# Cross-attention loop of a fused decoder layer: key and value units of two rounds issued in one block of the even round

## The chip, the cores and the metric

One NeuronCore of a Trainium2 chip runs the whole layer. The metric is the device time of one execution in microseconds (us); the kernel before was timed three times, and one further execution was profiled. The engines are named as the profile names them: PE (TensorE, with PEld for its weight loads), DVE (VectorE), ACT (ScalarE), POOL (GpSimd) and SP (SyncE, which here only issues transfers).

## What is computed

One pre-norm decoder layer on x (4 batches, 256 tokens, 128 channels): a local attention, a cross attention to a context of 512 tokens per batch, and two mixtures of 12 experts. The change lies in the cross attention, which per batch is, cut to what matters:

```python
lat = layer_norm(latents, ln_lat_g, ln_lat_b)
ctx = layer_norm(context, ln_ctx_g, ln_ctx_b)
q = (lat @ Wq).reshape(b, n, HEADS, DHEAD).transpose(0, 2, 1, 3)
k, v = jnp.split(ctx @ Wkv, 2, axis=-1)
k = apply_rope(k, cos, sin)
attn = jnp.einsum('bhnd,bhsd->bhns', q, k) * scale
attn = jax.nn.softmax(jnp.clip(attn, -11.0, 11.0), axis=-1)
out = jnp.einsum('bhns,bhsd->bhnd', attn, v) @ Wo + bo
```

There are 16 heads of 64 channels in each of 4 batches.

## The kernel before

The kernel writes one instruction stream per engine by hand, with semaphores between them. The cross attention is a loop of 32 rounds (`NPAIR`); a round is one pair of heads of one batch, and all five engines have their own copy of the loop. What the engines do in round r, in the order of their streams:

- **PE** (loop from L1311): the scores of the next pair, `scores(2r+2)` and `scores(2r+3)` (L1200, 16 matmul records each round); then the units: one value unit (`unit`, L1005 to L1007: 128 context tokens times 8 heads, for a round four later), one key unit (`key_products`, L1016 to L1018: all 512 tokens of the pair r+6), and in even rounds the queries of four heads (`queries`, L1134 to L1136); then the weighted values of this pair (`weigh_values`, L1219) and the sums of its weights (`sum_weights`, L1229). Units and queries use fp32r operands in three matmuls each (high and low parts), scores and values plain fp32.
- **ACT** (from L900): the exponentials of the next pair (`exponent`, L830, two of them), the copy of the value unit out of PSUM (`value_unit`, L739), in even rounds the copy of the queries (L821).
- **DVE** (from L1758): the division of the pair before (`divide`: reciprocal L1626, product L1630), the clips of the two exponentials (`clip`, L1619, in place), and the two reads of the key unit (`key_unit`: the sine part L1500, the cosine part L1505).
- **POOL** (from L611): two adds of the clipped weights (`weights_summed`, L573), one of the halves (`halves_summed`, L579), and the sum of the rotated key of pair r+4 (`key_sum`, L565), whose other half SP has swapped through SBUF by four transfers (`swap_halves`, L348).

What sets the order around the change are PSUM banks. Scores have banks 0 to 3, the outputs of pairs banks 4 and 7. **Bank 5** (`EXTRA_BANK`) takes the value units, and between them a turn of new latents or a projection of a finished batch (`extras`). **Bank 6** (`MISC_BANK`) takes the key units and the turned context of the next batch. `MISC` is the list of bank 6's users in order, and `misc_free(what)` makes PE wait until everything that stood in the bank before has been read:

```python
if MISC_NO[what]:
    pe.wait_ge(s["misc_read"], MISC_NO[what])
```

For a key unit the last read is DVE's cosine part L1505. In rounds 0, 6 and 14 the next batch's context is turned in bank 6 ahead of the key unit (`turn_context`, L979), read by ACT (`context_f`, L718, L724) and split by DVE (`context_lo`, L1491). In rounds 0 to 2, 9 to 11 and 14 to 16 DVE also normalizes the latents of the next batch in three parts (`latents`: statistics; L1445 and statistics; L1445), and POOL computes its square roots (L524, L525). Rounds 3, 12 and 17 end with the turn of these latents (L1112), rounds 11, 13, 19, 21, 27 and 29 with a projection (L1238) that DVE adds to x (`add_projected`, L1638). Rounds 22 on also carry the routing of the experts.

Of the kernel before, what the change touches and what calls it, by code (L numbers as in the profile page):

```python
# [7 lines left out]
P = 128  # L8
# [15 lines left out]
def decoder_layer(nc, x, ctx_in, pos, a_wq, a_wk, a_wv, a_wpost, a_wrel, a_pds,  # L24
# [77 lines left out]
    with ExitStack() as ctx:  # L102
# [115 lines left out]
        e_sb = sb("e_sb", [P, ERING, 2, KH, S], F32, second)  # L218
        v_sb.append(sb("v_sb1", [P, KC, HG, DX], F32, second))
        e_part = sb("e_part", [P, 2, 2, 2, S], F32, second)  # L220
# [68 lines left out]
        for r in range(NPAIR):  # L289
            if r + V_LEAD < NG * KC:  # L290
                ROUND_VALUES[r] = len(UNIT)
                UNIT.append(("v", r + V_LEAD))
# [10 lines left out]
        CONTEXT_ROUND = {0: 1, PPB - 2: 2, 2 * PPB - 2: 3}  # L303
# [17 lines left out]
        EXTRA_NO = {what: n for n, what in enumerate(EXTRA)}  # L321

# [189 lines left out]
        def _(pool):  # L512
# [137 lines left out]
        def _(act):  # L650
# [64 lines left out]
            def context_f(b):  # L715
                if b >= 1:
                    act.wait_ge(s["ctx_lo_done"], b)
                act.activation(ctx_f[:, :], bank(7 if b == 0 else MISC_BANK), ACT.Identity, scale=affine[:, 2:3], bias=affine[:, 3:4])\  # L718
                   .then_inc(s["misc_read" if b else "ctx_f_done"], 1)
                if b:  # L720
# [161 lines left out]
            outputs_turned(5)  # L882

# [16 lines left out]
            for r in range(NPAIR):  # L900
# [3 lines left out]
                if r in CONTEXT_ROUND:  # L904
                    misc_wait(("context", CONTEXT_ROUND[r]))
                    context_f(CONTEXT_ROUND[r])
                if r in ROUND_VALUES:
                    value_unit(ROUND_VALUES[r])
                if r % 2 == 0 and r // 2 + 1 < NQ:
                    queries_out(r // 2 + 1)  # L910
                if r in CONTEXT_NORM:
# [41 lines left out]
        def _(pe):  # L953
# [296 lines left out]
            local_project(2)  # L1250
            local_project(3)
# [46 lines left out]
            def route_1(i):  # L1298
                if i in ROUTE.values():
                    pe.wait_ge(s["v_done"], min(i // 2 + V_LEAD, NG * KC - 1) + 1)  # L1300
# [10 lines left out]
            for r in range(NPAIR):  # L1311
# [7 lines left out]
                if r in CONTEXT_ROUND:  # L1319
                    misc_free(("context", CONTEXT_ROUND[r]))  # L1320
                    turn_context(CONTEXT_ROUND[r], MISC_BANK, "misc_ps")
                if r in ROUND_VALUES:
                    route_read(2 * r - 2)
                    if extras.get(r - 1) in EXTRA_NO:
                        pe.wait_ge(s["extra_read"], EXTRA_NO[extras[r - 1]] + 1)
                    unit(ROUND_VALUES[r])
                if r + K_LEAD < NPAIR:
                    misc_free(("keys", r + K_LEAD))
                    key_products(r + K_LEAD, bank(MISC_BANK)).then_inc(s["misc_ps"], 1)
                if r % 2 == 0 and r // 2 + 1 < NQ:  # L1330
                    queries(r // 2 + 1)
                weigh_values(2 * r)
# [4 lines left out]
                if r in extras:  # L1337
                    what = extras[r]
                    if what in EXTRA_NO:
                        pe.wait_ge(s["v_done"], r + V_LEAD + 1)  # L1340
# [86 lines left out]
        def _(dve):  # L1427
# [313 lines left out]
            local_residual(3)  # L1741

# [7 lines left out]
            for r in range(NPAIR):  # L1750
                if r:
                    divide(r - 1)
                if r == NORM_ROUND:
# [11 lines left out]
                if r in CONTEXT_ROUND:  # L1765
                    context_lo(CONTEXT_ROUND[r])
# [4 lines left out]
                if r in extras:  # L1771
                    if extras[r][0] == "latents":
                        latents_lo(extras[r][1])
                    else:
                        add_projected(extras[r])
# [86 lines left out]
```

## Time and profile before

| | us |
|---|---|
| median of 3 runs (lowest to highest) | 430.64 (429.86 to 430.83) |
| the profiled execution, its own time | 430.4 |
| its span, first to last instruction | 428.5 |
| the loop: first scores of round 0 to the last values of round 31 | 61.50 to about 276.7 |
| busy in the span: PE, DVE, POOL, ACT | 402.4, 332.6, 260.0, 177.8 |

The granted TensorE clock is 1.00, the full 2.4 GHz, in every stretch. In a timeline row the first number is the start in us from the span's start, the second the duration, and a bracket at the end gives the idle time before the instruction with what ended it; rows of one kind that follow each other are merged, so "x2 1.92" is two instructions in 1.92 us. A matmul's duration contains its drain; the pace is read from start to start.

### The profile page before, as it was taken

How to read it: one execution, taken by the hardware profiler on the slowest of the kernel's cores; microseconds unless marked ns; L12 is line 12 of the kernel's file. 1: busy time of each engine (PE TensorE's matmuls, PEld its weight loads, DVE VectorE, ACT ScalarE, POOL GpSimd, SP SyncE). 2: the span in 40 equal slices, each digit the busy share in tenths (PEclk: the TensorE clock that was granted, in tenths of full speed). 3: DMA queues.
4: the chain of work that ended last, by engine and by line, in shares of the span. 5: the costliest groups of instructions: out<-in, count | busy, mean ns of one | idle time of the engine just before them, and what ended most of it. 6: DMA issues, size and time to landing. Idle time of an engine off the chain costs nothing.

```text
span 428.5 us, 8269 instructions
## 1 busy us (share of the span) xinstructions
PE 402.4 (94%) x3040; PEld 294.8 (69%) x3040; DVE 332.6 (78%) x655; ACT 177.8 (41%) x282; POOL 260.0 (61%) x225
## 2 busy tenths in 40 slices
PE   3988798989999999989999998999999999999996
PEld 2666675656677776757676675687767888888885
DVE  8888768998999978997788997886778861755544
ACT  6867354454464335443355435335257533000000
POOL 6823539999798988998979777767434850000000
PEclk9999999999999999999999999999999999999999
DMA  7696432131211111111201161547337730000000
GB/s 179 160 214 102 79 81 54 45 83 47 51 26 49 27 49 33 41 46 34 50 24 41 36 115 40 154 70 155 61 95 164 152 61 2 6 7 14 6 6 14
DMA packets 84746, 28.63 MB, mean 67 GB/s; under 512 B 71957, under 2 KB 79050, under 8 KB 84706
## 3 DMA queue, kind: packets, MB, share of 16 engines
q1 hardware_dynamic: 81748, 26.80, 28.3%
q10 hardware_dynamic: 2958, 1.30, 1.3%
q8 instruction: 25, 0.41, 0.4%
q14 instruction: 15, 0.12, 0.1%
HBM read 17.67 MB, written 2.02 MB: 46 GB/s over the span
## 4 chain that ended last, share of the span: by engine, by line
PE 66%; DVE 16%; SPq 7%; issue 4%; ACT 2%; DMA 2%; POOL 2%; DVEq 0%; ACTq 0%; POOLq 0%
PE psum L1219 10%; PE psum L1200 9%; PE psum L1402 5%; PE psum L1403 5%; PE psum L1401 5%; SPq L415 5%; PE psum L1362 4%; PE psum L1364 4%; PE psum L1363 4%; DVE rden L1626 4%; PE psum L1238 3%; PE psum L1229 3%; DVE e_sb L1619 2%; PE psum L1005 2%; PE psum L972 1%
## 5 line engine op out<-in xcount | busy, mean ns | idle before, releaser
L573 POOL TENSOR_TENSOR e_part<-e_sb 128x512 f32<-128x512 f32 x64 | 90.6, 1434 | 20.4 <-DVE e_sb L1619 20.4
L830 ACT ACTIVATE e_sb<-psum 128x1024 f32<-128x1024 f32 x64 | 62.2, 1022 | 85.0 <-PE psum L1200 82.9
L1200 PE MATMUL psum<-q_t,kT 64*128 64x256 f32 x512 | 64.2, 389 | 0.0
L1219 PE MATMUL psum<-e_sb,v_sb 128*64 128x256 f32 x512 | 63.8, 386 | 0.0
L1626 DVE RECIPROCAL rden<-psum 128x256 f32<-128x256 f32 x32 | 55.9, 1748 | 9.6 <-PE psum L1229 9.4
L1826 DVE SCALAR_TENSOR_TENSOR x_sb<-psum,dw,x_sb 128x128 f32<-128x128 f32 x96 | 33.7, 351 | 38.1 <-PE psum L1403 35.5
L1619 DVE TENSOR_SCALAR e_sb<-e_sb 128x1024 f32<-128x1024 f32 x64 | 58.6, 948 | 2.8 <-ACT e_sb L830 2.6
L1200 PEld LDWEIGHTS psum<-q_t,kT 64*128 64x128 f32 x512 | 46.7, 186 | 13.9 <-issue 8.4
L1219 PEld LDWEIGHTS psum<-e_sb,v_sb 128*64 128x64 f32 x512 | 33.7, 136 | 22.3 <-issue 6.3
L565 POOL TENSOR_TENSOR kT<-kT,raw 128x512 f32<-128x512 f32 x32 | 44.1, 1377 | 8.1 <-DMA raw<-rope_b 8.1
L602 POOL TENSOR_TENSOR xeT_lo<-xeT,xeT_hi 128x512 fp32r<-128x512 f32 x24 | 31.4, 1309 | 28.4 <-ACT xeT_hi L844 28.3
L579 POOL TENSOR_TENSOR e_part<-e_part 128x512 f32<-128x512 f32 x32 | 41.8, 1306 | 2.5
L1362 PE MATMUL psum<-xeT_hi,w1T_hi 128*128 128x512 f32 x96 | 38.9, 405 | 0.8 <-ACT h_f L946 0.5
L1402 PE MATMUL psum<-w2T_lo,h_hi 128*128 128x512 f32 x96 | 38.0, 396 | 0.0
L1403 PE MATMUL psum<-w2T_hi,h_lo 128*128 128x512 f32 x96 | 37.8, 394 | 0.0
L1364 PE MATMUL psum<-xeT_hi,w1T_lo 128*128 128x512 f32 x96 | 37.5, 391 | 0.0
L1363 PE MATMUL psum<-xeT_lo,w1T_hi 128*128 128x512 f32 x96 | 37.5, 390 | 0.0
L1401 PE MATMUL psum<-w2T_hi,h_hi 128*128 128x512 f32 x96 | 37.3, 389 | 0.0
L844 ACT ACTIVATE xeT_hi<-xeT 128x512 fp32r<-128x512 f32 x24 | 15.2, 632 | 29.4 <-DVE xeT L1669 21.3
L1362 PEld LDWEIGHTS psum<-xeT_hi,w1T_hi 128*128 128x128 f32 x96 | 18.0, 188 | 7.0 <-issue 2.6
L1500 DVE TENSOR_TENSOR rope_b<-psum,sinT 128x512 f32<-128x512 f32 x30 | 20.4, 679 | 2.1 <-PE psum L1018 2.1
L1505 DVE TENSOR_TENSOR kT<-psum,cosT 128x512 f32<-128x512 f32 x32 | 21.6, 676 | 0.0
(202 smaller groups left out, 729.9 us busy)
## 6 DMA issues: line engine op xcount, KB each, us to landing
raw<-rope_b SPq DMA_DIRECT2D x116, 64.0 KB, 2.0
w_raw<-in_L_ffn_W_dram SPq DMA_DIRECT2D x96, 64.0 KB, 2.3
gates<-gate_dram SPq DMA_DIRECT2D x6, 768.0 KB, 4.4
ctx_sb<-in_ctx_dram SPq DMA_DIRECT2D x4, 256.0 KB, 6.1
vbd<-v_dram SPq DMA_DIRECT2D x16, 52.6 KB
v_dram<-v_tok SPq DMA_DIRECT2D x4, 136.0 KB
raw<-in_L_xattn_Wkv_dram SPq DMA_DIRECT2D x2, 256.0 KB, 5.7
kT<-in_L_xattn_Wkv_dram SPq DMA_DIRECT2D x2, 256.0 KB, 4.7
```

Of the source, the lines that this page charges most:

```text
L573: pool.tensor_tensor(e_part[:, p % 2, half, :, :], e_sb[:, i % ERING, :, 0, :], e_sb[:, i % ERING, :, 1, :], ALU.add)\
L830: act.activation(e_sb[:, i % ERING, :, :, :].rearrange("p a k t -> p (a k t)"), psum[:, a:a + 2, :].rearrange("p a b -> p (a b)"), ACT.Exp ...
L1200: mm = pe.matmul(psum[:, 2 * (i % 2) + a, t * S:(t + 1) * S], key_slot(p)[rows, kt * P:(kt + 1) * P], q_t[rows, j % 2, p % 2, :], start=Tr ...
L1219: mm = pe.matmul(psum[DX * a:DX * a + DX, pv_bank(p), 0:S], v_sb[g % 2][:, kt, 2 * pp + a, :], e_sb[:, i % ERING, a, t, :], start=(kt == 0 ...
L1362: pe.matmul(bank(c), w1T_hi[:, e, c, :], hi, start=(e == 0), stop=False)
L1363: pe.matmul(bank(c), w1T_hi[:, e, c, :], lo, start=False, stop=False)
L1364: mm = pe.matmul(bank(c), w1T_lo[:, e, c, :], hi, start=False, stop=(e == NE - 1))
L1401: pe.matmul(o, hi, w_hi, start=(c == 0), stop=False)
L1402: pe.matmul(o, hi, w_lo, start=False, stop=False)
L1403: mm = pe.matmul(o, lo, w_hi, start=False, stop=(c == HC - 1))
L1619: dve.tensor_scalar(e, e, E_LO, E_HI, ALU.max, ALU.min).then_inc(s["clip_done"], 1)
L1626: dve.reciprocal(rden[:, p % 2, :], psum[:, pv_bank(p), S:2 * S]).then_inc(s["rden_done"], 1)
```

## The change

- Key and value units of rounds r and r+1 (r even) stand in round r. PE's even round becomes scores, value unit, key unit, queries, second value unit, second key unit, weighted values, sums. Its odd round has scores, weighted values and sums only.
- ACT copies the second value unit behind the queries of the even round; DVE does the reads of both key units one after the other behind the clips of the even round.
- Context 1 is turned ahead of the loop, in bank 6, behind `local_project(2)`. Contexts 2 and 3 are still turned in rounds 6 and 14, but behind the second key unit and in bank 5; DVE's `context_lo` for them stands in the round after.
- DVE adds a projection, or splits the latents' low part, behind the division of the round after, not ahead of it (save the last ones).
- Ahead of the loop, POOL's first sums of weights stand between the key sums, and no longer wait for all of x; for that two tiles (`e_part`, `v_sb1`) change places in memory.

```diff
-        for r in range(NPAIR):
-            if r + V_LEAD < NG * KC:
-                ROUND_VALUES[r] = len(UNIT)
-                UNIT.append(("v", r + V_LEAD))
+        for r in range(0, NPAIR - V_LEAD, 2):
+            ROUND_VALUES[r] = len(UNIT)
+            UNIT.extend([("v", r + V_LEAD), ("v", r + V_LEAD + 1)])
...
-        CONTEXT_ROUND = {0: 1, PPB - 2: 2, 2 * PPB - 2: 3}
+        CONTEXT_ROUND = {PPB - 2: 2, 2 * PPB - 2: 3}
...
-        MISC, EXTRA = [("queries", 0)], []
+        MISC, EXTRA = [("queries", 0), ("context", 1)], []
         for r in range(NPAIR):
             if r in CONTEXT_ROUND:
-                MISC.append(("context", CONTEXT_ROUND[r]))
-            if r + K_LEAD < NPAIR:
-                MISC.append(("keys", r + K_LEAD))
+                EXTRA.append(("context", CONTEXT_ROUND[r]))
+            if r % 2 == 0 and r + K_LEAD < NPAIR:
+                MISC.extend([("keys", r + K_LEAD), ("keys", r + K_LEAD + 1)])
...
-            for p in range(4):
-                key_sum(p)
-            pool.wait_ge(s["x1_done"], NT)
+            pool.wait_ge(s["lat_in_done"], TPB)
+            key_sum(0)
+            key_sum(1)
             weights_summed(0)
+            key_sum(2)
             weights_summed(1)
             halves_summed(0)
+            key_sum(3)
...
             local_project(2)
+            turn_context(1, MISC_BANK, "misc_ps")
             local_project(3)
...
-                if r in CONTEXT_ROUND:
-                    misc_free(("context", CONTEXT_ROUND[r]))
-                    turn_context(CONTEXT_ROUND[r], MISC_BANK, "misc_ps")
                 if r in ROUND_VALUES:
...
                     unit(ROUND_VALUES[r])
-                if r + K_LEAD < NPAIR:
+                if r % 2 == 0 and r + K_LEAD < NPAIR:
                     misc_free(("keys", r + K_LEAD))
                     key_products(r + K_LEAD, bank(MISC_BANK)).then_inc(s["misc_ps"], 1)
                 if r % 2 == 0 and r // 2 + 1 < NQ:
                     queries(r // 2 + 1)
+                if r in ROUND_VALUES:
+                    unit(ROUND_VALUES[r] + 1)
+                if r % 2 == 0 and r + K_LEAD < NPAIR:
+                    misc_free(("keys", r + K_LEAD + 1))
+                    key_products(r + K_LEAD + 1, bank(MISC_BANK)).then_inc(s["misc_ps"], 1)
+                if r in CONTEXT_ROUND:
+                    pe.wait_ge(s["v_done"], values_by(r))
+                    turn_context(CONTEXT_ROUND[r], EXTRA_BANK, "extra_ps")
...
                 if r:
                     divide(r - 1)
+                if extras.get(r - 1, "none")[0] == "project" and r - 1 < NPAIR - 3:
+                    add_projected(extras[r - 1])
...
-                if r + K_LEAD < NPAIR:
+                if r % 2 == 0 and r + K_LEAD < NPAIR:
                     key_unit(r + K_LEAD, MISC_BANK)
+                    key_unit(r + K_LEAD + 1, MISC_BANK)
```

How the instructions stand on PE from the units of an even round on, before (round 4 and the units of round 5; the lines are those of the kernel before):

```order
L1016 MATMUL psum<-ctx_hi,wkv_hi 128x512 [waits ctx_lo_done,misc_read]
...
L1136 MATMUL psum<-lat_hi,wq_lo 128x256
L1219 MATMUL psum<-e_sb,v_sb 64x256 [waits ox_done,v_done,clip_done]
...
L1200 MATMUL psum<-q_t,kT 128x256 x3
L1005 MATMUL psum<-wkv_hi,ctx_hi 128x512 [waits ctx_lo_done,v_done]
L1006 MATMUL psum<-wkv_lo,ctx_hi 128x512
L1007 MATMUL psum<-wkv_hi,ctx_lo 128x512
L1016 MATMUL psum<-ctx_hi,wkv_hi 128x512 [waits ctx_lo_done,misc_read]
L1017 MATMUL psum<-ctx_lo,wkv_hi 128x512
L1018 MATMUL psum<-ctx_hi,wkv_lo 128x512
```

and in the changed kernel (round 4 and the start of round 5; L1021 to L1023 are the value unit, L1032 to L1034 the key unit, L1150 to L1152 the queries, L1235 the weighted values):

```order
L1032 MATMUL psum<-ctx_hi,wkv_hi 128x512 [waits ctx_lo_done,misc_read]
...
L1152 MATMUL psum<-lat_hi,wq_lo 128x256
L1021 MATMUL psum<-wkv_hi,ctx_hi 128x512 [waits ctx_lo_done,v_done]
L1022 MATMUL psum<-wkv_lo,ctx_hi 128x512
L1023 MATMUL psum<-wkv_hi,ctx_lo 128x512
L1032 MATMUL psum<-ctx_hi,wkv_hi 128x512 [waits ctx_lo_done,misc_read]
L1033 MATMUL psum<-ctx_lo,wkv_hi 128x512
L1034 MATMUL psum<-ctx_hi,wkv_lo 128x512
L1235 MATMUL psum<-e_sb,v_sb 64x256 [waits ox_done,v_done,clip_done]
```

The second value and key unit moved up from the odd round, behind the queries; the second key unit waits on the same `misc_read` that DVE raises after the first.

On DVE, rounds 10 and 11 before (a round's rows are from its reciprocal to the next one):

```order
L1626 RECIPROCAL rden<-psum 128x256 [waits ox_done,den_ps]
L1630 TENSOR_TENSOR o_t<-psum,rden 128x256 [waits rden_done]
...
L1619 TENSOR_SCALAR e_sb<-e_sb 128x1024 [waits exp_done] x2
L1500 TENSOR_TENSOR rope_b<-psum,sinT 128x512 [waits keys_done,misc_ps]
L1505 TENSOR_TENSOR kT<-psum,cosT 128x512 [waits score_ps]
L1638 TENSOR_TENSOR x_sb<-psum,x_sb 128x128 [waits extra_ps]
L1626 RECIPROCAL rden<-psum 128x256 [waits ox_done,den_ps]
```

and in the changed kernel from the clips of round 10 on (L1644 is the clip, L1525 and L1530 the reads of a key unit, L1651 and L1655 the division, L1663 the added projection):

```order
L1644 TENSOR_SCALAR e_sb<-e_sb 128x1024 [waits exp_done] x2
L1525 TENSOR_TENSOR rope_b<-psum,sinT 128x512 [waits keys_done,misc_ps]
L1530 TENSOR_TENSOR kT<-psum,cosT 128x512 [waits score_ps]
L1525 TENSOR_TENSOR rope_b<-psum,sinT 128x512 [waits keys_done,misc_ps]
L1530 TENSOR_TENSOR kT<-psum,cosT 128x512 [waits score_ps]
...
L1651 RECIPROCAL rden<-psum 128x256 [waits ox_done,den_ps]
L1655 TENSOR_TENSOR o_t<-psum,rden 128x256 [waits rden_done]
L1663 TENSOR_TENSOR x_sb<-psum,x_sb 128x128 [waits extra_ps]
L1644 TENSOR_SCALAR e_sb<-e_sb 128x1024 [waits exp_done] x2
```

Both key units are read behind the clips of the even round, and the projection is added behind the division.

## Rows read from the trace of the kernel before

**Rows 1.** Rounds 6 to 17: PE, PEld, DVE, ACT, POOL busy, granted clock, DMA.

```profile
103.90:185.20 81.30, 80.19 (x586) 56.16 (x584) 74.98 (x101) 37.87 (x52) 72.14 (x56) 1.00 0.15 38
```

**Rows 2.** Timeline of PE, round 5 and the units of round 6.

```profile
98.08 2.00 PE L1200 MATMUL psum<-q_t,kT 64*128 64x256 f32 x16
100.01 0.50 PE L1005 MATMUL psum<-wkv_hi,ctx_hi 128*128 128x512 f32 x1
100.35 0.40 PE L1006 MATMUL psum<-wkv_lo,ctx_hi 128*128 128x512 f32 x1
100.58 0.39 PE L1007 MATMUL psum<-wkv_hi,ctx_lo 128*128 128x512 f32 x1
...
101.59 1.95 PE L1219 MATMUL psum<-e_sb,v_sb 128*64 128x256 f32 x16
103.90 2.00 PE L1200 MATMUL psum<-q_t,kT 64*128 64x256 f32 x16
...
107.75 0.51 PE L1016 MATMUL psum<-ctx_hi,wkv_hi 128*128 128x512 f32 x1 [0.56 <-ACT ctx_f L718]
...
108.56 0.28 PE L1134 MATMUL psum<-lat_hi,wq_hi 128*128 128x256 f32 x1
...
109.35 1.95 PE L1219 MATMUL psum<-e_sb,v_sb 128*64 128x256 f32 x16
```

**Rows 3.** Who PE waited for, 61.5 to 274.7 us: us in total, times, longest.

```profile
PE psum L1134 <- DVE o_t L1630: 4.8, 5, 1.5
PE psum L1016 <- ACT ctx_f L718: 1.7, 3, 0.6
PE psum L1229 <- POOL e_part L579: 1.0, 1, 1.0
```

**Rows 4.** Timeline of PE and ACT: score starts of rounds 19, 20, 25; exponentials of 19.

```profile
193.13 2.00 PE L1200 MATMUL psum<-q_t,kT 64*128 64x256 f32 x16
...
200.96 2.00 PE L1200 MATMUL psum<-q_t,kT 64*128 64x256 f32 x16
...
236.19 2.00 PE L1200 MATMUL psum<-q_t,kT 64*128 64x256 f32 x16
...
194.31 1.94 ACT L830 ACTIVATE e_sb<-psum 128x1024 f32<-128x1024 f32 x2 [2.78 <-PE psum L1200]
```

**Rows 5.** Timeline of DVE, rounds 19, 20 and 25.

```profile
195.38 1.92 DVE L1619 TENSOR_SCALAR e_sb<-e_sb 128x1024 f32<-128x1024 f32 x2
...
197.83 0.67 DVE L1505 TENSOR_TENSOR kT<-psum,cosT 128x512 f32<-128x512 f32 x1
...
205.32 0.68 DVE L1505 TENSOR_TENSOR kT<-psum,cosT 128x512 f32<-128x512 f32 x1
...
239.35 1.69 DVE L1619 TENSOR_SCALAR e_sb<-e_sb 128x1024 f32<-128x1024 f32 x1 [0.22 <-ACT e_sb L830]
...
241.56 0.67 DVE L1505 TENSOR_TENSOR kT<-psum,cosT 128x512 f32<-128x512 f32 x1
```

**Rows 6.** Timeline of POOL and DVE around round 17's clips (182.30), one instruction a row.

```profile
181.51 1.29 POOL L579 TENSOR_TENSOR e_part<-e_part 128x512 f32<-128x512 f32 x1
182.30 1.05 DVE L1619 TENSOR_SCALAR e_sb<-e_sb 128x1024 f32<-128x1024 f32 x1
182.76 1.72 POOL L565 TENSOR_TENSOR kT<-kT,raw 128x512 f32<-128x512 f32 x1
...
183.27 1.76 DVE L1619 TENSOR_SCALAR e_sb<-e_sb 128x1024 f32<-128x1024 f32 x1
```

**Rows 7.** POOL's adds, 95 to 240 us: shortest, median, longest in ns.

```profile
L573 POOL TENSOR_TENSOR e_part<-e_sb x43: 1257/1277/1797, 95.6 to 239.2; 128x512 f32<-128x512 f32 x43
```

**Rows 8.** Timeline of DVE, parts of the latents' normalization, and round 0's clips.

```profile
132.10 2.30 DVE L1445 TENSOR_SCALAR xn<-x_sb,mv,rstd 128x128 f32<-128x128 f32 x2
...
175.19 1.57 DVE L1445 TENSOR_SCALAR xn<-xn,mv,rstd 128x128 f32<-128x128 f32 x2
...
63.73 3.19 DVE L1619 TENSOR_SCALAR e_sb<-e_sb 128x1024 f32<-128x1024 f32 x2 [0.31 <-ACT e_sb L830]
```

More of the change, by code:

```diff
@@ L218, in decoder_layer @@
         e_sb = sb("e_sb", [P, ERING, 2, KH, S], F32, second)
+        e_part = sb("e_part", [P, 2, 2, 2, S], F32, second)
         v_sb.append(sb("v_sb1", [P, KC, HG, DX], F32, second))
-        e_part = sb("e_part", [P, 2, 2, 2, S], F32, second)
         rden = sb("rden", [P, 2, S], F32, second)
@@ L288, in decoder_layer, with values_by @@
         ROUND_VALUES = {}
-        for r in range(NPAIR):
-            if r + V_LEAD < NG * KC:
-                ROUND_VALUES[r] = len(UNIT)
-                UNIT.append(("v", r + V_LEAD))
+        for r in range(0, NPAIR - V_LEAD, 2):
+            ROUND_VALUES[r] = len(UNIT)
+            UNIT.extend([("v", r + V_LEAD), ("v", r + V_LEAD + 1)])
+        def values_by(r):
+            return min(r - r % 2 + V_LEAD + 2, NG * KC)
         UNIT_BANK += [5] * (len(UNIT) - len(UNIT_BANK))
@@ L321, in decoder_layer, with extra_before @@
         EXTRA_NO = {what: n for n, what in enumerate(EXTRA)}
+        def extra_before(r):
+            at = [EXTRA_NO[what] for q in range(r) for what in (("context", CONTEXT_ROUND.get(q)), extras.get(q)) if what in EXTRA_NO]
+            return max(at, default=-1) + 1
         def key_slot(p):
@@ L717, in context_f @@
                     act.wait_ge(s["ctx_lo_done"], b)
-                act.activation(ctx_f[:, :], bank(7 if b == 0 else MISC_BANK), ACT.Identity, scale=affine[:, 2:3], bias=affine[:, 3:4])\
-                   .then_inc(s["misc_read" if b else "ctx_f_done"], 1)
-                if b:
+                act.activation(ctx_f[:, :], bank((7, MISC_BANK, EXTRA_BANK, EXTRA_BANK)[b]), ACT.Identity, scale=affine[:, 2:3], bias=affine[:, 3:4])\
+                   .then_inc(s[("ctx_f_done", "misc_read", "extra_read", "extra_read")[b]], 1)
+                if b >= 2:
+                    act.wait_ge(s["extra_read"], EXTRA_NO["context", b] + 1)
+                elif b:
                     act.wait_ge(s["misc_read"], MISC_NO["context", b] + 1)
@@ L882, in _ @@
             outputs_turned(5)
+            misc_wait(("context", 1))
+            context_f(1)
             def context_normalize(b):
@@ L903, in _ @@
                     exponent(2 * r + 3)
-                if r in CONTEXT_ROUND:
-                    misc_wait(("context", CONTEXT_ROUND[r]))
-                    context_f(CONTEXT_ROUND[r])
                 if r in ROUND_VALUES:
@@ L910, in _ @@
                     queries_out(r // 2 + 1)
+                if r in ROUND_VALUES:
+                    value_unit(ROUND_VALUES[r] + 1)
+                if r in CONTEXT_ROUND:
+                    act.wait_ge(s["extra_ps"], EXTRA_NO["context", CONTEXT_ROUND[r]] + 1)
+                    context_f(CONTEXT_ROUND[r])
                 if r in CONTEXT_NORM:
@@ L1299, in route_1 @@
                 if i in ROUTE.values():
-                    pe.wait_ge(s["v_done"], min(i // 2 + V_LEAD, NG * KC - 1) + 1)
+                    pe.wait_ge(s["v_done"], values_by(i // 2))
                 if i == ROUTE["weights"]:
@@ L1339, in _ @@
                     if what in EXTRA_NO:
-                        pe.wait_ge(s["v_done"], r + V_LEAD + 1)
+                        pe.wait_ge(s["v_done"], values_by(r))
+                        if EXTRA_NO[what]:
+                            pe.wait_ge(s["extra_read"], EXTRA_NO[what])
                     else:
@@ L1741, in _ @@
             local_residual(3)
+            context_lo(1)
             beside = {6: (output_bias, 0), NPAIR - 6: (output_bias, 1)}
@@ L1760, in _ @@
                     clip(2 * r + 3)
-                if r + K_LEAD < NPAIR:
+                if r % 2 == 0 and r + K_LEAD < NPAIR:
                     key_unit(r + K_LEAD, MISC_BANK)
+                    key_unit(r + K_LEAD + 1, MISC_BANK)
                 if r == NORM_ROUND:
                     final_norm(0, 1)
-                if r in CONTEXT_ROUND:
-                    context_lo(CONTEXT_ROUND[r])
+                if r - 1 in CONTEXT_ROUND:
+                    context_lo(CONTEXT_ROUND[r - 1])
                 if r in beside:
@@ L1770, in _ @@
                 route_1(2 * r)
[L1771 to L1775, printed above, removed]
+                if extras.get(r - 1, "none")[0] == "latents":
+                    latents_lo(extras[r - 1][1])
+                if r in extras and r >= NPAIR - 3:
+                    add_projected(extras[r])
                 route_1(2 * r + 1)
```

8 lines of the change are left out of this document (5 added, 3 removed).

## The prediction

> **What bounds the kernel now.** I read the busy time by stretch first. In rounds 6 to 17 PE is busy 80.2 of 81.3 us, DVE 75.0 and POOL 72.1, the clock at its full 2.4 GHz [rows 1]. So the loop is PE's, with two engines close behind. PE's timeline then gives the cost of a round. Scores take 1.93 us (98.08 to 100.01), the units of an odd round 1.58 (to 101.59), weighted values and sums 2.31 (to 103.90) [rows 2]. Inside the units a matmul of 512 columns follows the one before by 0.23 (100.35 to 100.58), so a unit is 0.70; the queries are 0.70 too (108.56 to 109.35 is 0.79, with the way out below). Six matmuls would be 1.40, so going from fp32 into fp32r and back costs 0.18 per round, 0.11 of it on the way in (100.01 to 100.35 against 0.23) [rows 2]. Last, the list of waits: in the loop PE waits for the division 4.8 us in five places, for a turned context 1.7 in three, once 1.0 for the first sums [rows 3]. After a wait the first unit takes 0.81 and not 0.70 (107.75 to 108.56) [rows 2], so I add 0.1 to each.
>
> **What is taken away.**
> - *Blocks.* Rounds 1, 3, ... 27, fourteen of them, lose their way in and out: 14 x 0.18 = 2.5.
> - *Contexts.* The three waits go, since context 1 is turned in a gap ahead of the loop and the others behind the units: 1.7 + 0.3 = 2.0. The transposes themselves stay.
> - *Division first.* The queries of an even round wait for the division of the pair before. DVE's odd round is now shorter by one key unit, and an added projection no longer stands ahead of the division: 4.8 + 0.5 = 5.3, if all five waits go.
> - *First sums.* POOL does them between the key sums: 1.0.
>
> Together 10.8. POOL's, ACT's and SP's work is the same; the swaps of a key are issued a round earlier or later, with four rounds until POOL needs it, and cost nothing. The exchanged tiles cost nothing.
>
> **What is added.** PE's second key unit writes bank 6, and `misc_free` holds it until DVE has finished the cosine part of the first. Before, that read had a whole round; now it has what stands between the two key units on PE, queries and a value unit, 1.40 us. Behind the waiting unit on PE stand this pair's weighted values and sums and the next scores; behind those wait DVE's next division and ACT's next exponentials. So every us of this wait is a us of the loop, in the 13 rounds 0, 2, ... 24.
>
> Without a wait the second key unit would start 1.93 + 0.11 + 4 x 0.70 = 4.84 us after the round's scores. When is DVE done? In its order stand division, two clips, two reads. In round 19, where DVE had been idle, the clips start 2.25 after the scores (195.38 against 193.13), the exponentials 1.18 after (194.31), and the cosine part ends at 198.50, 5.37 after [rows 4, 5]. Round 20 is the shortest with 5.04 (200.96 to 206.00), round 25 the longest with 6.04 (236.19 to 242.23) [rows 4, 5]. All are later than 4.84. With 0.06 for the signal and 0.1 for the restart the wait costs at least 5.04 + 0.06 - 4.84 + 0.1 = **0.36** and by these rows at most 1.36.
>
> I expect more, because clips and POOL's adds exclude each other. A clip alone takes 0.60; in round 17 the first was issued at 182.30, ran only when POOL's add ended at 182.80, and the second stood from 183.27 to 185.03, until POOL's next add had ended at 184.48 [rows 6]. That add took 1.72 where 1.28 is the median of POOL's adds [rows 6, 7]. They take turns. In round 25 the second clip came 0.22 after the first and waited for an add too: 1.69 [rows 5].
>
> Now the cycle. In the odd round POOL has long been idle, so its four adds start behind the first clip, at 2.25 + 0.65 = 2.9 after the scores; with 0.6 for the second clip and 4 x 1.25 they end at 8.5. The odd round lasts only 1.93 + 2.31 = 4.24 on PE, so POOL adds until 4.3 us into the even round, across both clips. That is round 17's pattern: 2.73 for the pair of clips (182.30 to 185.03). Issued at 2.25 they end at 4.98, the two reads take 1.28 and end at 6.26, and the wait costs 6.26 + 0.06 - 4.84 + 0.1 = 1.6; a second clip of the odd round that runs late as in round 25 pushes the division by up to 0.45, which makes 2.0. I take the middle.
> - Rounds 4, 6, 8, 18, 24, behind a short odd round: 5 x 1.8 = 9.0.
> - Rounds 12, 14, 20, 22, behind an odd round with a projection (2 us longer, in which POOL catches up and only one add is in the way, as in round 25): 6.04 gives 1.36, so 4 x 1.4 = 5.6.
> - Rounds 2, 10, 16, where a part of the latents' normalization (1.6 to 2.3, with its statistics up to 3.0 [rows 8]) stands ahead of the clips on DVE; some 0.9 of it falls into time that DVE would wait for the second exponential: 3 x 3.0 = 9.0.
> - Round 0: clips of 3.2 us among POOL's key sums, 63.73 to 66.92, now behind the context's low part [rows 8]; with the reads 68.2, 6.7 after the scores at 61.5, with that part about 7.3: 2.5.
>
> Sum 26.1.
>
> The Trainium skill says in SBUF — State Buffer, section SBUF: two separate sides, that VectorE and GpSimd share one pair of ports under an exclusive lock, so that the one that comes second waits for the other's whole instruction. The rows of round 17 agree, 1.05 and 1.76 us against 0.60. By the rule, with every clip behind a full add, the five plain rounds would cost 2.0 and the sum would be 1.0 higher.
>
> **Sum.** 430.4 + 26.1 - 10.8 = 445.7 against the profiled execution; the median of the runs lies 0.2 above it, so **445.9**. Break-even is a mean wait of 10.8 / 13 = 0.83 us. Ends: with 0.36 in all 13 rounds 430.6 - 10.8 + 4.7 = 424.5; with 2.1, 1.9, 3.5 and 3.0 in the four groups (31.6) and one division wait left in round 2 (0.8), 452.2.
>
> **Rivals.**
> - *The cover nearly holds* (faster). The mechanism is the same place, `misc_free` ahead of the second key unit, with DVE at its earliest: POOL's adds fall between the clips, and the cosine part ends about 5.0 after the scores as in round 20. Then the wait is 0.36 and the time 424 to 429. It decides below 0.83. For it: DVE has 1.3 us more to itself in odd rounds. Against: three of three rounds read have 5.04 or more with POOL less late than it will be.
> - *The wait is that of the rows of before.* POOL's lag does not carry over, and the mean of 5.04, 5.37 and 6.04, 5.48, holds: 0.8 in nine rounds, 2.0 in the three with normalization, 2.5 in round 0, 15.7 in all: 435.5. This is no change or a little slower, around 430 to 438.
> - *The clock falls.* The Trainium skill says in TensorE: Matmul & The Clock Gate, The HAM clock gate, that an array left idle long enough runs at half speed until it has been busy again. As a mechanism here: the longest waits, about 3 us in rounds 2, 10 and 16, would be followed by the rest of their round (0.70 + 2.31) at 1.2 GHz, 3 us more each, and so 455. The rows show 1.00 with waits of up to 1.5 [rows 1, 3]; longer ones inside the loop no row here shows.
>
> That the change does not do what it says can be left out: the streams show the second units in the even round.
>
> **How the numbers follow.** Forecast 0.58 (438 to 452); the rows' own wait 0.24 (430 to 438); the cover nearly holds 0.13; the clock 0.05. The range 429 to 452 leaves out most of the third, the clock and the edges, about 0.2. A measurement of this kernel tells about 0.2% (0.9 us) from no change: faster 0.14, same 0.05, slower 0.81.
>
> **What would show it.** In the changed profile PE's list of waits should have the second key unit waiting for DVE's cosine part, some 13 times and about 25 us, as its largest entry, no wait for a turned context, and little for the division. In the timeline an even round should last 9.5 to 10 us and an odd one 4.2, and the clips of even rounds should stand behind POOL's adds. I am wrong if that wait is under 0.8 a round, if PE's odd rounds wait for something, or if the clock is under 1.00.

## The result, and the profile after

The changed kernel takes **454.42 us** (median of 4 runs, 452.91 to 456.61) against 430.74 of the kernel before (429.86 to 433.42): ratio 1.0543, 95% interval 1.0479 to 1.0606. Forecast were 445.9 and at most 452. The profiled execution took 456.61, its span is 454.7.

Two lines of the page after, busy time and the granted clock in 40 slices:

```profile
PE 411.7 (91%) x3040; PEld 298.0 (66%) x3040; DVE 334.5 (74%) x655; ACT 179.8 (40%) x282; POOL 256.9 (56%) x225
...
PEclk9999998899898899989999999999999999999999
```

PE is busy 9.3 us longer (402.4 before) with the same number of matmuls, DVE and ACT about 2 us longer, POOL 3 us less; the 8s are slices in which the clock fell. Who PE waited for, in the whole execution (us in total, times, longest):

```profile
PE psum L1032 <- DVE kT L1530: 22.5, 12, 4.2
...
PE psum L1150 <- DVE o_t L1655: 2.2, 2, 1.7
```

Against [rows 3]: the turned context and the first sums are gone, of the 4.8 us for the division 2.2 are left (rounds 26 and 28), and the key unit has come in as the largest entry: 21.9 us in ten rounds of the loop, the other two waits stand ahead of it. In rounds 14, 20 and 22 the second key unit is 0.27 us late, which the list does not count. One even round, PE's timeline from the second value unit of round 8 to the end of round 9 (start, duration):

```profile
131.41 0.40 PE L1021 MATMUL psum<-wkv_hi,ctx_hi 128*128 128x512 f32 x1
...
134.34 0.50 PE L1032 MATMUL psum<-ctx_hi,wkv_hi 128*128 128x512 f32 x1 [2.08 <-DVE kT L1530]
...
135.25 3.43 PE L1235 MATMUL psum<-e_sb,v_sb 128*64 128x256 f32 x16
...
139.24 2.00 PE L1216 MATMUL psum<-q_t,kT 64*128 64x256 f32 x16
141.17 1.95 PE L1235 MATMUL psum<-e_sb,v_sb 128*64 128x256 f32 x16
```

Two losses follow each other: 2.08 us of waiting, and then weighted values that take 3.43 us where they take 1.95 in round 9. Why the cosine part was late, DVE and POOL in round 8:

```profile
130.38 2.70 DVE L1644 TENSOR_SCALAR e_sb<-e_sb 128x1024 f32<-128x1024 f32 x2
133.01 0.68 DVE L1525 TENSOR_TENSOR rope_b<-psum,sinT 128x512 f32<-128x512 f32 x1
133.61 0.68 DVE L1530 TENSOR_TENSOR kT<-psum,cosT 128x512 f32<-128x512 f32 x1
...
129.55 1.29 POOL L587 TENSOR_TENSOR e_part<-e_part 128x512 f32<-128x512 f32 x1
130.80 1.73 POOL L573 TENSOR_TENSOR kT<-kT,raw 128x512 f32<-128x512 f32 x1
```

The two clips take 2.70 us among POOL's adds, as in [rows 6], and the reads stand behind them. Granted clock of whole rounds (length; PE, PEld, DVE, ACT, POOL busy; clock; share and GB/s of the DMA), rounds 4, 8 and 9, and 10, and last a stretch inside the weighted values of round 8:

```profile
96.88:106.55 9.67, 8.21 (x56) 5.62 (x55) 8.09 (x10) 4.61 (x7) 9.21 (x7) 1.00 0.12 29
...
127.14:139.24 12.10, 10.03 (x56) 6.27 (x55) 8.40 (x10) 5.16 (x9) 10.10 (x8) 0.86 0.09 22
139.24:143.48 4.24, 4.24 (x39) 2.81 (x37) 4.01 (x8) 1.94 (x2) 1.13 (x1) 1.00 0.26 66
143.48:156.62 13.14, 9.85 (x57) 6.37 (x55) 9.32 (x14) 3.62 (x5) 12.36 (x11) 0.87 0.08 20
...
136.00:138.00 2.00, 2.00 (x12) 1.09 (x10) 0.64 (x2) 0.00 (x0) 2.00 (x2) 0.50 0.01 1
```

Rounds 0, 2, 6, 8, 10 and 16 read 0.86 to 0.88, all others 1.00. The 0.50 is 1.2 GHz. From the second key unit to the next scores five of the six need 4.80 to 4.90 us, where rounds 4, 18 and 20 with 1.00 need 3.20 to 3.22; round 6, which also turns a context, needs 5.28 where round 14 needs 3.64: **1.65 us each, 9.9 in all.** Ahead of the second key unit each of the six had waited 1.84 to 4.16 us; round 4 waited 1.46 and kept its clock. The Trainium skill (TensorE: Matmul & The Clock Gate, The HAM clock gate) has it that an array left idle runs at half rate until it has been busy again; the 0.50 above agrees, and 16 matmuls in 3.43 for 1.95 us are near that.

**Where the time went**, from round 0's scores to round 30's (208.83 us before, 234.66 after): the second key unit starts 24.6 us later than it could (4.84 after the round's scores), summed over 13 rounds; 1.3 for the restarts; 9.9 for the clock; less 2.5 for the blocks. That leaves 7.5 for everything else taken away: 234.66 - 208.83 = 25.9 + 9.9 - 2.5 - 7.5. The 2.5 is the forecast's own figure and the 7.5 a remainder. Compared pair by pair of rounds, with the late start, the restart and the slow stretch taken off, the blocks give 0.20 in each of 14 pairs (2.8), the three contexts 2.2 and 0.4 more because the transposes of context 1 left the loop, the first sums 1.3, the division 3.3: together 10.0. A wait costs more than the list shows: round 4 of the kernel before lasts 8.17 us and round 8, which has none, 6.54, for a listed wait of 1.40.

### The profile page after: what moved, and what is told of

The parts are those of the page before. It is cut to its first block, busy times and chain, and to the rows that moved or that the text cites. A ratio compares the mean times of both kernels' runs of the same rounds, so it can differ in the third digit from the quotient of the medians.

```text
span 454.7 us, 8275 instructions
## 1 busy us (share of the span) xinstructions
PE 411.7 (91%) x3040; PEld 298.0 (66%) x3040; DVE 334.5 (74%) x655; ACT 179.8 (40%) x282; POOL 256.9 (56%) x225
## 4 chain that ended last, share of the span: by engine, by line
PE 58%; DVE 26%; issue 7%; ACT 4%; DMA 2%; ACTq 1%; POOL 1%; DVEq 0%; POOLq 0%
PE psum L1235 11%; PE psum L1216 6%; DVE e_sb L1644 6%; DVE rden L1651 5%; PE psum L1427 5%; PE psum L1428 5%; PE psum L1426 5%; PE psum L1387 4%; PE psum L1388 4%; PE psum L1389 4%; PE psum L1254 3%; PE psum L1245 2%; DVE xn L1470 2%; DVE rope_b L1525 2%; DVE kT L1530 2%
## 5 line engine op out<-in xcount | busy, mean ns | idle before, releaser
L581 POOL TENSOR_TENSOR e_part<-e_sb 128x512 f32<-128x512 f32 x64 | 87.6, 1381 | 46.0 <-DVE e_sb L1644 45.4
L1651 DVE RECIPROCAL rden<-psum 128x256 f32<-128x256 f32 x32 | 56.1, 1752 | 23.8 <-PE psum L1245 23.7
L1235 PE MATMUL psum<-e_sb,v_sb 128*64 128x256 f32 x512 | 71.9, 424 | 0.0
L1644 DVE TENSOR_SCALAR e_sb<-e_sb 128x1024 f32<-128x1024 f32 x64 | 65.3, 1043 | 7.0 <-ACT e_sb L842 6.9
L1235 PEld LDWEIGHTS psum<-e_sb,v_sb 128*64 128x64 f32 x512 | 37.1, 150 | 29.1 <-issue 17.2
L1032 PE MATMUL psum<-ctx_hi,wkv_hi 128*128 128x512 f32 x32 | 14.6, 457 | 23.0 <-DVE kT L1530 22.5
L1525 DVE TENSOR_TENSOR rope_b<-psum,sinT 128x512 f32<-128x512 f32 x30 | 20.6, 685 | 15.8 <-PE psum L1034 15.8
L1032 PEld LDWEIGHTS psum<-ctx_hi,wkv_hi 128*128 128x128 f32 x32 | 6.0, 187 | 30.4 <-DVE kT L1530 29.2
```

The source lines that it names most:

```text
L581: pool.tensor_tensor(e_part[:, p % 2, half, :, :], e_sb[:, i % ERING, :, 0, :], e_sb[:, i % ERING, :, 1, :], ALU.add)\
L1235: mm = pe.matmul(psum[DX * a:DX * a + DX, pv_bank(p), 0:S], v_sb[g % 2][:, kt, 2 * pp + a, :], e_sb[:, i % ERING, a, t, :], start=(kt == 0 ...
L1644: dve.tensor_scalar(e, e, E_LO, E_HI, ALU.max, ALU.min).then_inc(s["clip_done"], 1)
L1651: dve.reciprocal(rden[:, p % 2, :], psum[:, pv_bank(p), S:2 * S]).then_inc(s["rden_done"], 1)
```

## The experiments

The front part of the kernel, ahead of the loop, differs by up to 2.5 us between the profiled executions (the loop began at 59.89 to 62.44), and the number of rounds in which the clock fell does too (the same kernel, e3 below: span 428.0 us at a mean clock of 1.000, 434.0 at 0.984). So mechanisms are compared by the stretch from round 0 to 30 of the profiled executions, and kernels by their medians. The ratios of e1 to e11 are to executions of the kernel before made beside them, with medians of 431.1 to 431.4 and mean clocks of 0.991 to 0.999; 430.74 and 208.83 are of the executions of the result.

| kernel | median us | ratio to before (95%) | rounds 0 to 30 | mean clock |
|---|---|---|---|---|
| before | 430.74 | | 208.83 | 1.000 |
| as changed | 454.42 | 1.0543 (1.0479 to 1.0606) | 234.66 | 0.977 |
| e1 keys apart | 429.20 | 0.9951 (0.9930 to 0.9971) | 206.91 | 1.000 |
| e2 before, merged | 453.53 | 1.0562 (1.0487 to 1.0638) | 229.74 | 0.985 |
| e3 read first | 432.94 | 1.0047 (1.0010 to 1.0084) | 213.48 | 0.984 |
| e4 filled | 447.43 | 1.0381 (1.0335 to 1.0426) | 224.86 | 0.998 |
| e6 parts behind | 429.44 | 0.9967 (0.9945 to 0.9989) | 207.32 | 0.996 |
| e7 short adds | 430.50 | 0.9975 (0.9944 to 1.0006) | 206.91 | 1.000 |
| e8 key inside | 428.04 | 0.9928 (0.9908 to 0.9949) | 206.76 | 0.999 |
| e9 parts odd | 427.31 | 0.9909 (0.9878 to 0.9941) | 206.04 | 0.999 |
| e10 odd, last | 426.54 | 0.9895 (0.9857 to 0.9933) | 204.03 | 0.999 |
| e11 apart, odd, last | 429.58 | 0.9969 (0.9944 to 0.9995) | 208.04 | 0.998 |

### e1: all but the key units

```diff
-                if r % 2 == 0 and r + K_LEAD < NPAIR:
-                    misc_free(("keys", r + K_LEAD + 1))
-                    key_products(r + K_LEAD + 1, bank(MISC_BANK)).then_inc(s["misc_ps"], 1)
...
-                if r % 2 == 0 and r + K_LEAD < NPAIR:
-                    key_unit(r + K_LEAD, MISC_BANK)
-                    key_unit(r + K_LEAD + 1, MISC_BANK)
+                if r + K_LEAD < NPAIR:
+                    key_unit(r + K_LEAD, MISC_BANK)
```

> The changed kernel with the key units back in their own rounds, one per round; the value units of two rounds stay in one block, and the order on VectorE, the contexts and POOL's first sums stay as changed. Theory T (PE's second key unit waits for VectorE's cosine part in 13 rounds, 25.9 us with the restarts, and six of these waits are followed by a stretch at 1.2 GHz, 9.9 us): both go, 2.3 us of ways in and out of fp32r come back, and up to 2.9 us of waits for the division, since VectorE's odd rounds are longer again. 454.4 - 35.8 + 2.3 = 421 to 424 us, granted clock 1.00 in the loop, no entry for the key unit in PE's list of waits. Rival R1 (the loss comes from the parts that stay: two value units through one bank, contexts turned behind them, late added projections): 445 us or more. Between, 430 to 440, if both take part.

Measured: 429.20, above the 421 to 424 expected. The loss is gone with the key units' place, so R1 falls; but the other parts brought 1.9 us in the loop and not some 7. PE's waits in this kernel:

```profile
PE psum L1150 <- DVE o_t L1652: 4.6, 5, 1.5
PE psum L995 <- ACT v_sb L751: 1.4, 2, 0.7
```

The division's waits are as long as before, only elsewhere (0.31 in round 8 and 1.02 in round 16 are new, those of rounds 4 and 18 gone), and the contexts' transposes, now behind the second value unit in one bank with it, wait for ACT's copy of it.

### e2: nothing but the merged units

```diff
+        for r in range(0, NPAIR - V_LEAD, 2):
+            ROUND_VALUES[r] = len(UNIT)
+            UNIT.extend([("v", r + V_LEAD), ("v", r + V_LEAD + 1)])
...
+                if r % 2 == 0 and r + K_LEAD < NPAIR:
+                    misc_free(("keys", r + K_LEAD + 1))
+                    key_products(r + K_LEAD + 1, bank(MISC_BANK)).then_inc(s["misc_ps"], 1)
```

> The kernel before with nothing but the value and key units of two rounds in one block of the even round; VectorE's order, the contexts' place and bank and POOL's order stay as before. Theory T: 430.7 + 25.9 + 9.9 - 2.5 (fourteen blocks fewer) = 464 us, 460 or more in any case, with the key unit's wait as the largest entry. What the other three parts of the change are worth together is then the distance to 454.4, by the account of the two traces 5.9 us (contexts 2.0, division 2.9, first sums 1.0). Rival R1 (the loss is in the other parts): 428 to 440 us.

Measured: 453.53 (451.89 in the profiled execution, 458.38 at a mean clock of 0.972 in another), as slow as the whole change, so the merged units alone are the loss. It is less than expected for two reasons. In the profiled execution the clock fell in two rounds (2 and 16, behind 4.41 and 4.35 us) and not in six. In rounds 0, 6 and 8 the waits for DVE are shorter than as changed (0.30, 0.61 and 1.47 us). But round 10 waits as long as changed; PE there,

```profile
145.51 0.50 PE L1026 MATMUL psum<-ctx_hi,wkv_hi 128*128 128x512 f32 x1 [3.29 <-DVE kT L1523]
...
146.40 1.95 PE L1229 MATMUL psum<-e_sb,v_sb 128*64 128x256 f32 x16
```

keeps its pace behind 3.29 us. And waits of the kernel before vanish without the parts that were to remove them. In round 6 the context is still turned ahead of the units and waited for, and yet the second key unit starts 6.82 us after the scores, as changed 6.84: what PE waits for upstream is taken off the wait for DVE. Without the slow stretches (9.9 as changed, 4.2 here) the two loops are 224.8 and 225.5 us: with the keys merged, contexts, division and first sums together are worth 0.8.

### e3: the reads ahead of the clips

```diff
+                if r % 2 == 0 and r + K_LEAD < NPAIR:
+                    key_unit(r + K_LEAD, MISC_BANK)
                 if r + 1 < NPAIR:
                     clip(2 * r + 2)
                     clip(2 * r + 3)
                 if r % 2 == 0 and r + K_LEAD < NPAIR:
-                    key_unit(r + K_LEAD, MISC_BANK)
                     key_unit(r + K_LEAD + 1, MISC_BANK)
```

> The changed kernel, but VectorE reads the first key unit (sine and cosine part) ahead of its two clips in the even round; nothing is added or taken away. Theory T (the second key unit waits only because the two clips stand ahead of the reads and alternate with POOL's adds): the first key unit is done about 3.4 us after the round's scores, its two reads take 1.28, so bank 6 is free at 4.8 us, where the second key unit would start by itself at 4.84. Waits of 0.1 or less in plain rounds, up to 1 in the three with a part of the normalization and in round 0, none long enough for the clock to fall: 454.4 - 25.9 - 9.9 + 1 to 3 = 420 to 422 us. Rival R2 (the reads are late by themselves, since the division ahead of them or POOL's adds hold VectorE in any order): the waits stay at 10 us or more in all, 432 us or more. Rival R3 (the clips, now later, make POOL's sums late, and PE's sums of weights wait for them): the key unit's wait goes, but PE's list shows a wait of 5 us or more for POOL, 425 to 432 us.

Measured: 432.94 against 420 to 422 expected, with 21.2 us of the loop back by an order on DVE. In ten rounds the second key unit starts 4.96 to 5.13 after the scores (as changed 5.1 to 7.5). In rounds 2, 10 and 16 waits stayed, and there the expectation was too low: 2.12, 1.76 and 1.87 us, with a slow stretch behind each. Round 2 on DVE and PE:

```profile
78.50 2.74 DVE L1470 TENSOR_SCALAR xn<-xn,mv,rstd 128x128 f32<-128x128 f32 x2
81.16 0.68 DVE L1525 TENSOR_TENSOR rope_b<-psum,sinT 128x512 f32<-128x512 f32 x1
...
82.49 0.50 PE L1032 MATMUL psum<-ctx_hi,wkv_hi 128*128 128x512 f32 x1 [2.12 <-DVE kT L1530]
...
83.38 3.60 PE L1235 MATMUL psum<-e_sb,v_sb 128*64 128x256 f32 x16
```

The normalization's two instructions take 2.74 us here, 0.59 in round 11, where POOL has no add in hand. So T holds in ten rounds; the other three are late as R2 has it, though their waits are 5.8 us in all and not 10.

### e4: PE kept busy while it waits

```diff
+                if r in FILL_MM:
+                    pe.wait_ge(s["exp_done"], 2 * r + 3)
+                    for _ in range(FILL_MM[r]):
+                        pe.matmul(bank(0), wkv_hi[:, 0:P], ctx_hi[:, (r + K_LEAD) // PPB % 2, :], start=True, stop=True)
```

`FILL_MM = {0: 10, 2: 16, 6: 7, 8: 8, 10: 13, 16: 17}`.

> The changed kernel with 71 matmuls whose result nobody reads (512 columns, written to a score bank after its exponential) put into the six long waits of rounds 0, 2, 6, 8, 10 and 16, 7 to 17 of 0.23 us in each, fewer than the wait holds; they only keep PE busy. Theory T (the waits themselves and the stretches at 1.2 GHz behind the long ones are two separate losses): the waits stay, the clock is 1.00 in all rounds, and 9.9 us come back: about 444.5 us, up to 447 where a faster round lets VectorE be later for the next. Rival R4 (the slow stretches cost nothing, since VectorE and POOL set the pace of these rounds, and what PE gains it waits in the next key unit): 452 to 456 us with the clock at 1.00 and PE's waits, filled ones counted, longer by 8 us or more.

Measured: 447.43, and 9.80 us less in the loop than as changed, 9.9 expected. The medians are only 7.0 apart, since the profiled execution of the changed kernel was the slowest of its four and the one of e4 the fastest. Rounds 8 and 10 with the fill:

```profile
121.36:131.76 10.40, 10.13 (x64) 7.04 (x62) 8.40 (x10) 5.16 (x9) 9.62 (x8) 1.00 0.11 27
136.00:147.52 11.52, 11.17 (x69) 8.07 (x67) 9.33 (x14) 3.63 (x5) 11.21 (x10) 1.00 0.09 23
```

The clock is 1.00, and the second key units start where they did, 7.20 and 8.32 us after the scores (7.20 and 8.30 as changed). Work that nobody needs saves 9.8 us: the two losses are separate, and R4 falls.

### e6: the latents' parts behind the clips

```diff
-                    if r in rounds:
+                    if r % 2 and r in rounds:
                         latents(b, rounds.index(r))
...
+                for b, rounds in LATENT_ROUNDS.items():
+                    if r % 2 == 0 and r in rounds:
+                        latents(b, rounds.index(r))
```

> The kernel with the reads of the first key unit ahead of the clips, and in the even rounds 0, 2, 10 and 16 the part of the latents' statistics and normalization on VectorE behind the clips too (POOL's square roots of these rounds behind its sums); nothing is added or taken away. In the run before this one the three waits left, 2.12, 1.76 and 1.87 us, stand in rounds 2, 10 and 16, where such a part stands ahead of the reads, and each is followed by 1.65 us at 1.2 GHz. Theory T: these 5.7 + 5.0 us go, 432.9 - 10.7 = 422 us, granted clock 1.00, up to 425 where the division of rounds 3, 11 and 17 gets late. Rival R3 (what is put off makes something else late: POOL's sums, the turned latents or the division): new waits of 1 to 2 us in those rounds, 426 to 429 us.

Measured: 429.44 against 422 to 425 expected. The three waits and their slow stretches are gone, but waits of R3's kind stand in five rounds: for the division 0.96, 1.25, 0.82 and 0.87 us in rounds 2, 8, 16 and 18, and 1.31 in round 12 for the projection that DVE adds behind its put-off work. The expected 422 forgot that DVE's time is only moved.

### e7: POOL's adds on an eighth of the columns

```diff
+                n = S if p < 2 else S // 8
-                pool.tensor_tensor(e_part[:, p % 2, half, :, :], e_sb[:, i % ERING, :, 0, :], e_sb[:, i % ERING, :, 1, :], ALU.add)\
+                pool.tensor_tensor(e_part[:, p % 2, half, :, 0:n], e_sb[:, i % ERING, :, 0, 0:n], e_sb[:, i % ERING, :, 1, 0:n], ALU.add)\
```

The adds of the halves and, from pair 4 on, those of the rotated keys are cut short in the same way.

> The changed kernel with POOL's adds of pairs 2 and up on an eighth of their columns; the sums of weights and the rotated keys lack the rest, everything else runs as changed. VectorE's order stays as changed, clips ahead of the reads. Theory T (VectorE's clips and normalizations are long because they and POOL's adds exclude each other): a pair of clips takes 1.3 and not 2.7 to 2.9 us, the normalization 0.6 and not 2.3 to 2.7, so the cosine part ends at about 5.0 us after the scores in plain rounds: extra start of the second key unit 0.1 to 0.4 us there, 0.5 to 1.5 in rounds 2, 10 and 16, no fall of the clock: 454.4 - 25.9 - 9.9 + 3 to 6 = 421 to 425 us. Rival R5 (the clips are late because the exponentials are, and VectorE's own sequence of division, clips and reads is too long): the plain rounds keep 1 us or more each, 432 us or more.

Measured: 430.50 in the median of ten runs, above the 421 to 425 expected, and 426.72 in the profiled execution. Six of the ten had a mean clock of 0.988 to 0.996 and took 430.0 to 432.2, four had 0.999 or 1.000 and took 426.7 to 427.9; where the clock fell in the six no trace shows. The profiled loop, at 1.00, is 27.75 us shorter than as changed. DVE in round 8:

```profile
116.21 0.68 DVE L1647 TENSOR_SCALAR e_sb<-e_sb 128x1024 f32<-128x1024 f32 x1
117.08 0.77 DVE L1647 TENSOR_SCALAR e_sb<-e_sb 128x1024 f32<-128x1024 f32 x1 [0.19 <-ACT e_sb L845]
117.76 0.68 DVE L1528 TENSOR_TENSOR rope_b<-psum,sinT 128x512 f32<-128x512 f32 x1
...
128.79 0.59 DVE L1473 TENSOR_SCALAR xn<-x_sb,mv,rstd 128x128 f32<-128x128 f32 x2
```

The clips of round 8 end 1.6 us after the first was issued and not 2.7, and round 10's normalization takes 0.59 for 2.49. The second key unit is 0.3 late in plain rounds, 0.85, 1.25 and 1.46 in rounds 2, 10 and 16, and 2.66 as before in round 0, where the adds are still whole: 8.9 us in all for 24.6. So 15.7 us of the wait are POOL's adds, and 15.7 + 9.9 for the clock + 2.2 for the division, whose last waits went too, is 27.8. R5 falls. The Trainium skill's exclusive lock (SBUF — State Buffer, SBUF: two separate sides) fits: clips and normalizations grow beside adds, the reads of PSUM are 0.66 to 0.69 in every kernel.

### e8 and e9: is the block worth anything then

e8 puts the first key unit ahead of the last matmul of the first value unit, on top of e6:

```diff
+                if inside:
+                    inside()
                 return pe.matmul(o, lo, wkv_hi[:, wc:wc + GC], start=False, stop=True)
```

> The kernel of e6_parts_behind, and on PE the first key unit stands ahead of the last matmul of the first value unit, 0.23 us earlier, so that VectorE's reads of it (3.62 to 4.9 us after the scores where they come first) end before the second key unit wants the bank. Theory T (in that order the second key unit still came 0.13 us late in ten rounds and paid 0.11 for the restart): 13 x 0.24 = 3.1 us less than e6_parts_behind, about 419 us, and the second key unit starts at 4.84 after the scores. Rival R6 (the 0.24 us lie in the way from fp32r matmul to matmul of another bank, not in a wait): the same time as e6_parts_behind.

Measured: 428.04 against about 419 expected, 0.56 us less in the loop than e6, not 3.1. Plain even rounds take 8.17 in both. The lateness only changed its place: round 10, PE's last queries and second value unit, and ACT's copy of the first:

```profile
130.17 0.28 PE L1158 MATMUL psum<-lat_hi,wq_lo 128*128 128x256 f32 x1
130.43 0.49 PE L1025 MATMUL psum<-wkv_hi,ctx_hi 128*128 128x512 f32 x1
...
129.77 0.60 ACT L755 ACTIVATE v_sb<-psum 128x512 f32<-128x512 f32 x1 [0.50 <-PE psum L1029]
```

The queries' last matmul has a pace of 0.12, so the value unit could start at 130.29; it starts at 130.43, behind the copy, and pays the restart. In a block of five units one of the two banks is read 0.13 to 0.14 us too late in either order.

e9 keeps e3's order and moves the latents' parts by their table:

```diff
-        LATENT_ROUNDS = {1: (0, 1, 2), 2: (9, 10, 11), 3: (14, 15, 16)}
+        LATENT_ROUNDS = {1: (0, 1, 3), 2: (7, 9, 11), 3: (13, 15, 17)}
```

> The kernel with the reads of the first key unit ahead of the clips, and the latents' parts in other rounds by their table: 0, 1, 3 and 7, 9, 11 and 13, 15, 17 instead of 0, 1, 2 and 9, 10, 11 and 14, 15, 16, so that no part but the first stands in an even round. Theory T: the waits of rounds 2, 10 and 16 go with their slow stretches, as in e6_parts_behind: 422 to 425 us. Rival R7 (an odd round is 4.2 us short and VectorE has no room in it: the part makes the next division or the next reads late): waits for the division or the key unit of 1 us or more in rounds 4, 8, 10, 12, 14, 16 and 18, 428 us or more.

Measured: 427.31, between what T and R7 expect: no wait for the key unit is left, but waits for the division of 0.39 to 0.87 us in rounds 2, 4, 6, 10 and 18.

### e10 and e11: the best order, merged and apart

```diff
-                if r % 2 == 0 and r // 2 + 1 < NQ:
+                if r != NPAIR - 4 and r % 2 == 0 and r // 2 + 1 < NQ:
                     queries(r // 2 + 1)
...
                 weigh_values(2 * r)
+                if r == NPAIR - 4:
+                    queries(r // 2 + 1)
```

Both kernels have this edit and e9's table; e10 has e3's order on DVE too, e11 the key units of e1 in its place.

> The kernel of e9_parts_odd (reads of the first key unit ahead of the clips, the latents' parts in odd rounds), and the last queries, of round 28, stand behind the first half of that round's weighted values instead of ahead of them. In e9_parts_odd they wait 1.68 us for the division of round 27 with nothing else to do on PE; the half of the weighted values takes 0.89 us and needs no division of that round. Theory: the division ends 0.9 us later than PE can take the queries then, or less: 0.9 to 1.5 us less than e9_parts_odd, about 426 us, which is 4 to 5 us below the kernel before. Rival R8 (the queries' way to SBUF is late for the next scores instead): the same as e9_parts_odd, 427.3 us.

> The same two edits (latents' parts in odd rounds, last queries behind half of the weighted values) on the kernel with the key units apart, one per round. It differs from e10_odd_last in the main part of the change alone: key units of two rounds in one block or not, with every long wait gone from both. Theory T (in one block a way in and out of fp32r is saved, 0.18 us, but the second key unit comes 0.13 us late behind the reads even where they come first and pays 0.11 for the restart, so that a pair of rounds takes 12.41 us merged and 12.36 apart): 13 x 0.05 = 0.7 us and less between the two, the one with keys apart not slower by itself; its odd rounds keep VectorE busier, so waits for the division of 0.3 to 1 us may come back in some even rounds. 425 to 428 us. Rival (blocks are worth the 2.5 us that the prediction gave them): this one is slower than e10_odd_last by 2 us or more.

Measured: 426.54 and 429.58. e10 is the fastest of this study, 1.05% below the kernel before (0.7 to 1.4%), and 4.8 us in the loop, where neither profile shows a fall of the clock: the queries' wait in round 28 is gone, and that round lasts 6.00 us for 7.55 in e9, so R8 falls. The 3.0 us between e10 and e11 (4.0 in the profiled loops) meet the rival's number and not its reason. A pair of rounds without waits takes 12.41 merged and 12.36 apart, so the blocks give nothing. What differs are waits, first of e10, then of e11:

```profile
PE psum L1150 <- DVE o_t L1657: 3.1, 6, 0.7
```

```profile
PE psum L1150 <- DVE o_t L1654: 5.0, 7, 1.3
PE psum L995 <- ACT v_sb L751: 1.4, 2, 0.7
```

Merged, DVE has its odd round free for the division, and the second key unit stands between ACT's copy and the transposes: 1.9 + 1.4 us. But the 3.0 are not all the merged units': e9's table is made for odd rounds without a key unit, which e11 does not have. Against e1, whose parts stand as before, e11 gains 1.54 us in round 28 and still has a loop 1.13 longer. With e1's table and the late queries the kernel apart would have, as an estimate from these two traces, 206.91 - 1.54 = 205.4, 1.3 behind e10; it was not run.

## Why the prediction was wrong

- **The mechanism of the wait was right, and its sum came out by luck.** `misc_free` ahead of the second key unit waits for DVE's cosine part: 26.1 us forecast, 24.6 + 1.3 measured. Odd rounds of 4.24 us came out to the hundredth. Clips and normalizations behind POOL's adds are the larger part of it (e7: 15.7 of 24.6), and the order on DVE alone takes 16.2 of the 24.6 away (e3). The sum is luck because two of its four groups were off and cancel (below).
- **The step that failed is the clock.** The prediction named it as a rival with 5%, 3 us in each of rounds 2, 10 and 16, and left it out of the sum because the rows showed 1.00 with waits of up to 1.5. Its own sum had waits of 3 in three rounds and 2.5 in a fourth, longer than any row of the loop, so the rows did not speak for 1.00 there, and the upper end of 452 was built without it. The clock fell in six rounds at 1.65 each, 9.9 us (e4 takes them back). With it the forecast would have been 455.8. That the rival's 455 comes as near is luck: it named half as many rounds at nearly twice the price.
- **Two groups were mis-sized and cancel** (extra start and restart). Behind a projection 5.6 forecast, 1.5 measured: POOL's last add ended at 165.60, half a us into the first of round 12's clips (165.07), and none stood in the way of the second. In rounds 2, 10 and 16 9.0 forecast, 12.3 measured: the normalization excludes the adds too, 2.49 for 0.59. Plain rounds 9.0 and 9.3, round 0 2.5 and 2.8.
- **What was taken away was right in the sum, wrong in the parts.** 10.8 forecast, 10.0 found, the division with 3.3 for 5.3. But the three parts that were to bring 8.3 bring 0.8 on the merged kernel (e2) and 1.9 with the key units apart (e1): most of those waits are covered by the new one, or come back elsewhere.
- **The rows read for the end of the cosine part were not the trace's range.** Rounds 20 and 25, called the shortest and the longest, have 5.04 and 6.04 us after the scores, and with round 19 they gave the rival of the rows' own wait its mean of 5.48. In the 17 rounds of the kernel before that have a key unit and no part of the normalization the trace has 5.05 to 7.45, with a mean of 6.25 (round 12, for one, 6.45), so that rival was priced too low.
- The blocks' 0.18 us a round is right on PE and still worth nothing, since the second key unit is 0.13 late even at best and restarts for 0.11 (e3, e8).

## What to carry to other kernels

When two users of one buffer are moved together, compare what stands between them on the writer with what the reader has to do first, in its own order; here 1.40 us stood against 1.28 of reads and 2.7 of clips that nobody needed so early, and exchanging the two gave 21 us back. When a forecast contains idle times longer than any row shows, put a half-rate stretch behind each (1.65 us here) at least into the upper end of the range. And do not add up waits that lie one behind the other in one round: the last one absorbs the others.

## What was not expected of the hardware

- How long PE waits does not by itself decide whether the clock falls: 1.76 us in e3 were followed by a slow stretch, 3.29 in e2 were not, and the mean clock of one kernel differed from execution to execution (e3, 0.984 to 1.000). The kernel before, at 1.000 in its profile, had 0.991 to 0.999 in its later executions. What decides it was not tried further and stays open.
- Two normalizations of 128 x 128 on DVE, 0.59 us by themselves, take 2.5 to 2.7 beside POOL's adds: in round 2 of e3 the two end at 79.89 and 81.24, each 0.1 behind the end of an add (79.80 and 81.15).
- A second key unit that comes 0.13 us late for a semaphore costs 0.24 (nine rounds of e3, at 4.96 to 4.98): the matmul behind its first follows by 0.34 and not by 0.23.
